# One Perceiver layer on one core: the heads' content stored by single tiles, the exponential's table loaded later, eleven zero products, one rounding moved

## The reference

```python
x = x + xattn(layernorm(x), ctx)      # Q = x Wq' + bq, K = ctx Wk' + bk, softmax(Q K'/32) ctx; ctx has 4096 rows
x = x + attn(layernorm(x), ...)       # 128 heads of 8, latent 128, rope part of 64
x = x + ffn(layernorm(x), W1, b1, W2, b2)

# attn
c_q = x @ Wq_down;  c_kv = x @ Wkv_down
q_c = (c_q @ Wq_up).reshape(b, s, 128, 8);  q_r = (x @ Wq_rope).reshape(b, s, 128, 64)
k_c = (c_kv @ Wk_up).reshape(b, s, 128, 8); v_c = (c_kv @ Wv_up).reshape(b, s, 128, 8)
k_r = x @ Wk_rope
scores = (einsum(q_c, k_c) + einsum(q_r, k_r)) / sqrt(72)
out = (softmax(scores) @ v_c).reshape(b, s, 1024) @ Wo

# ffn: two of these, W1 of 4096 x 1024 and W2 of 1024 x 4096
outlier = max(abs(x), axis=rows) > 3
y = quant_rows(where(outlier, 0, x)) @ quant_rows(W).T + where(outlier, x, 0) @ W.T + b
# quant_rows: scale = max(max|row|/127, 1e-8); round(a/scale) * scale
```

## Time and profile before

| | |
|---|---|
| median of three runs | 924.37 us (923.29 to 924.41) |
| profiled execution, whole time | 925.35 us |
| its span in the profile | 923.3 us |
| busy: PE, PEld | 895.4 us (97%), 818.6 us (89%) |
| busy: DVE, ACT, POOL | 684.6, 627.3, 488.9 us (74, 68, 53%) |
| mean granted PE clock | 0.994 |

### The profile page before, as it was taken

How to read it: one execution, slowest core, us unless ns; L and a number is a source line. 1 busy time by engine, 2 the same in 40 slices (tenths; PEclk the granted TensorE clock), 3 DMA queues, 4 the chain that set the end, 5 groups by cost and what they waited for, 6 DMA issues and landing times.

```text
span 923.3 us, 19052 instructions
## 1 busy us (share of the span) xinstructions
PE 895.4 (97%) x6866; PEld 818.6 (89%) x6866; DVE 684.6 (74%) x1090; ACT 627.3 (68%) x1093; POOL 488.9 (53%) x334
## 2 busy tenths in 40 slices
PE   8999999999999899999999999999899999999997
PEld 6997888888887789999999999987689999899997
DVE  6447676768456468888888888996888888887754
ACT  5424444465444568888888888986678787878762
POOL 0220000045443797777778777773176676376673
PEclk9999999999999999999999999999999999999999
DMA  8566756678754779566565655556232433224221
GB/s 327 190 206 237 293 207 273 249 267 318 275 202 147 221 228 307 174 195 193 179 190 177 213 176 190 176 192 199 93 137 97 178 128 145 92 93 164 109 92 46
DMA packets 80696, 174.82 MB, mean 189 GB/s; under 512 B 7632, under 2 KB 57584, under 8 KB 78064
## 3 DMA queue, kind: packets, MB, share of 16 engines
q1 hardware_dynamic: 79920, 173.63, 53.8%
q10 hardware_dynamic: 704, 0.23, 0.1%
HBM read 161.51 MB, written 11.53 MB: 187 GB/s over the span
## 4 chain that ended last, share of the span: by engine, by line
PE 73%; DVE 6%; ACT 4%; POOL 3%; issue 2%; DMA 2%; SPq 0%; DVEq 0%; ACTq 0%; POOLq 0%
PE bank L51 17%; PE bank L53 17%; PE bank L52 17%; PE bank L1408 4%; PE bank L1409 3%; PE bank L549 3%; PE bank L1379 3%; PE bank L1804 2%; PE bank L2089 2%; PE bank L1424 2%; POOL W_all L2328 1%; DMA ring<-in_L_attn_Wq_rope_dram 1%; POOL wl L1003 1%; PE bank L1391 1%; PE bank L731 1%
## 5 line engine op out<-in xcount | busy, mean ns | idle before, releaser
L1003 POOL TENSOR_TENSOR wl<-ring,wh 128x1024 fp32r<-128x1024 f32 x68 | 161.9, 2402 | 0.0
L51 PE MATMUL bank<-act_all,W_all 128*128 128x256 f32 (+1 forms) x512 | 154.0, 301 | 2.3 <-POOL W_all L2328 1.9
L51 PE MATMUL bank<-act_all,wh 128*128 128x256 f32 x512 | 144.5, 282 | 1.3 <-DVE qq L1609 0.9
L52 PE MATMUL bank<-act_all,wh 128*128 128x256 f32 x512 | 144.1, 281 | 0.0
L53 PE MATMUL bank<-act_all,W_all 128*128 128x256 f32 (+1 forms) x512 | 144.0, 281 | 0.0
L53 PE MATMUL bank<-act_all,wl 128*128 128x256 f32 x512 | 143.8, 281 | 0.0
L513 POOL TENSOR_TENSOR xa_WT_l<-ring,xa_WT_h 128x1024 fp32r<-128x1024 f32 x16 | 43.4, 2732 | 176.6 <-ACT xa_WT_h L508 166.7
L2328 POOL TENSOR_TENSOR W_all<-rnd,W_all 128x512 fp32r<-128x512 f32 x72 | 92.3, 1292 | 57.4 <-ACT W_all L2215 52.1
L1616 DVE TENSOR_TENSOR pl<-bank,ph 128x512 f16<-128x512 f32 x128 | 88.1, 688 | 44.4 <-ACT ph L1555 41.6
L1000 POOL CAST wh<-ring 128x1024 fp32r<-128x1024 f32 x68 | 68.8, 1041 | 69.5 <-PE bank L53 62.2
L51 PEld LDWEIGHTS bank<-act_all,W_all 128*128 128x128 f32 x512 | 97.1, 190 | 3.4 <-POOL W_all L2328 2.5
(11 more groups left out here) (275 smaller groups left out, 2604.2 us busy)
## 6 DMA issues: line engine op xcount, KB each, us to landing
ring<-in_ctx_dram SPq DMA_DIRECT2D x16, 2048.0 KB, 8.1
ring<-in_L_attn_Wq_rope_dram SPq DMA_DIRECT2D x32, 1024.0 KB, 6.4
ring<-in_L_ffn_W_dram SPq DMA_DIRECT2D x14, 2048.0 KB, 7.7
panel<-in_L_ffn_W_dram SPq DMA_DIRECT2D x48, 512.0 KB, 4.6
w1p<-in_L_ffn_W_dram SPq DMA_DIRECT2D x16, 512.0 KB, 3.7
ring<-in_L_xattn_Wq_dram SPq DMA_DIRECT2D x2, 2048.0 KB, 12.5
ring<-in_L_xattn_Wk_dram SPq DMA_DIRECT2D x2, 2048.0 KB, 7.8
ring<-in_L_attn_Wo_dram SPq DMA_DIRECT2D x4, 1024.0 KB, 5.0
```

Source lines behind the costliest of these rows:

```text
L51: pe.matmul(out, lh, rh, start=start, stop=False, skip_group_check=True)
L52: pe.matmul(out, lh, rl, start=False, stop=False, skip_group_check=True)
L1003: pool.tensor_tensor(half_of(l, i), half_of(r, i), f32(half_of(h, i)), ALU.subtract).then_inc(w_lo, 1)
```

## The change

Four edits.

1. Content. Before the heads only the keys of buffer 0 are spread, and only the first tile of q and of k is stored (`store_tiles`, 128 KB a DMA). SP then reads group 0's content back, spreads the other two buffers, stores the second tile (on a semaphore of its own, for which group 4 waits), and only then loads piece 2 of Wq_rope.
2. The exponential's table is loaded behind the copies of the values.
3. Zero products in layer norm 3: 3 become 8 ahead of the first turned rows, 6 become 10 ahead of the masked rows, 5 become 7 ahead of the scaled rows.
4. First W1 step: DVE scales chunk 0's results one rounding later; ACT biases them behind k = 6 and 7, by a table of its own.

```diff
@@ content_sync and what it calls
+            stored_left = sem("stored_left")
+            def store_tiles(sp, i, tiles, done):
                 for s in range(SLOTS):
                     part = con_l if s == 2 - i else con_h
                     sp.dma_start(content_dram[i][tiles, s * P:(s + 1) * P, :].rearrange("t p q -> p t q"),
-                                 f32(part[i][:, tiles, :])).then_inc(stored[u], 16)
+                                 f32(part[i][:, tiles, :])).then_inc(done, 16)
+            def store_content(sp, u, i):
+                sp.wait_ge(con_lo, 2 * u + i + 1)
+                store_tiles(sp, i, slice(2 * u, 2 * u + 2), stored[u])
...
                     sp.wait_ge(kr_hi, 2)
-                    for b in range(QBUF):
-                        sp.dma_start(f32(kmix[0:ROPE, b * GROUP:(b + 1) * GROUP, :]),
-                                     f32(krope[0:ROPE, 1, :]).unsqueeze(1).to_broadcast([ROPE, GROUP, T])).then_inc(k_spread, 16)
+                    spread_keys(sp, 0)
                     for i in range(2):
-                        store_content(sp, 0, i)
-                    sp.wait_ge(k_spread, QBUF * 16)
+                        sp.wait_ge(con_lo, i + 1)
+                        store_tiles(sp, i, slice(0, 1), stored[0])
@@ content_scalar
-                    load_exp(act, ident[:, 0:1])
                     act.wait_ge(e_ready, 1)
...
                             act.activation(value_part(kt, h, 0), by_head(bank[2 * kt + h][:, :]), ACT.Copy).then_inc(v_hi, 1)
+                    load_exp(act, ident[:, 0:1])
@@ heads_sync
                         if g % 8 == 0:
                             sp.wait_ge(stored[g // 8], 2 * SLOTS * 16)
+                        elif g == 4:
+                            sp.wait_ge(stored_left, 2 * SLOTS * 16)
...
-                    next_w(2)
+                    sp.wait_ge(k_spread, 16)
+                    sp.wait_ge(cleared, 2 * QBUF + 1)
                     for g in range(FIRST, NG):
...
                         if valid(g + 2):
                             content(g + 2)
+                        if g == FIRST:
+                            for b in (1, 2):
+                                spread_keys(sp, b)
+                            for i in range(2):
+                                store_tiles(sp, i, slice(1, 2), stored_left)
+                            next_w(2)
+                            sp.wait_ge(k_spread, QBUF * 16)
@@ feed-forward tables, zero products, first step
-            TILES_AT_FIRST = ((), (), (), (), (0, 1), (2,), (3,), ())
+            TILES_AT_FIRST = ((), (), (), (), (), (0, 1), (2,), (3,))
+            BIASED_AT_FIRST = ((), (), (), (), (), (), (0,), (1, 2, 3))
...
-                        keep_warm(pe, 4, 3)
+                        keep_warm(pe, 4, 8)
...
-                        keep_warm(pe, 2, 6)
+                        keep_warm(pe, 2, 10)
                         for h in range(2):
                             pe.wait_ge(y_masked, 4 + 4 * h)
...
-                        keep_warm(pe, 2, 5)
+                        keep_warm(pe, 2, 7)
                         pe.wait_ge(m_max, 2 * QT)
...
-                    step(0, 0, None, None, first=True, tiles=TILES_AT_FIRST)
+                    step(0, 0, None, None, first=True, tiles=BIASED_AT_FIRST)
```

6 lines of the change are left out of this document (3 added, 3 removed).

## The result

The changed kernel takes **928.25 us** (median of six runs, 927.5 to 930.06), the kernel before beside it 924.39 us (six runs, 922.1 to 925.3): ratio 1.0047, 95% interval 1.0035 to 1.0058, so 3.9 us slower. Two repeats gave 1.0044 (1.0027 to 1.0061) and 1.0037 (1.0024 to 1.005). The forecast was 923.6 us with a range of 920.6 to 926.6; the result lies above it.

A forecast was written before the change was run, and what follows sets the result against it. PE, busy nearly throughout, was taken as the bound. Content +2.3, layer norm 3 -0.9 and W1 -2.2 sum to -0.8: profiled 925.35 becomes 924.55, or 923.6 us after the profiled run's 0.98 above the median; range 920.6 to 926.6.

The forecast's parts named there:

- Table: Start of the heads: without the exponential's table load ahead, PE starts the content products at 303.1 instead of 303.60, 0.5 us less.
- Content: Heads' start: the new transfer order delays the end of POOL's chain from 341.68 to 344.0, +2.3 us, between -0.2 and +4.7.
- POOL's chain of 20.6 us: Heads: fixed-order POOL work from Wq_rope piece 2's landing (321.05) to PE's restart (341.68), 20.6 us, sets the stage.
- The landing of w2: Heads: Wq_rope piece 2 (w2) lands at 323.4 instead of 321.05; bounds 320.9 and 325.8.
- The sum, 322.5: Heads: start of data movement at 312.2 plus transfer times of content, two spreads, six stores and Wq_rope piece 2 gives 322.5.
- the lag behind it: Heads: time from the summed transfers to Wq_rope piece 2's landing, taken as 0.9 us; it was 3.3 before.
- a new stretch at 0.50 behind 320: Sign anywhere behind 320 us: a new stretch at granted clock 0.50 would mean the prediction is wrong.
- PE's waits, 2 to 3 us in sum: Heads, 327 to 344: PE waits 2 to 3 us in sum for POOL's low part or group 1's content.
- rival B: Heads: Wq_rope piece 2 lands late, 1 us per us after 321.05; 926.0 us, with low clock 927.7; chance 0.15.
- rival A: Heads: transfers hidden, Wq_rope piece 2 lands at 321 or before; 921.1 us, 919.2 if at 319 or before; chance 0.26.
- Layer norm 3: Layer norm 3: added zero products hold the clock and DVE's 0.94 us wait goes, -0.9 us; bounds 0 and -0.94.
- W1: First W1 product: moved rounding, -0.85 from PE's wait, -1.65 from clock, +0.3 later maxima: -2.2 us; bounds -0.5 and -2.5.

The follow-up runs named there:

- after_again: The changed kernel itself, run again with a second profile: 927.77 us, ratio 1.0044 to the kernel before.
- w2_first: The changed kernel with Wq_rope piece 2 issued directly behind group 0's content, ahead of two spreads and the second tile's stores: 929.6 us, ratio 1.004.
- zeros_only: The kernel before with only layer norm 3's zero products changed: 924.17 us, ratio 0.9998.
- no_content: The changed kernel with the content's transfers as before, the other three edits kept: 922.89 us, ratio 0.997; its repeat 923.04 us, ratio 0.9992.
- w2_behind_content0: The kernel before, two-tile stores kept, with Wq_rope piece 2 issued behind group 0's content and SP's wait for the stores: 926.72 us, ratio 1.0025.
- w2_mid: The changed kernel with Wq_rope piece 2 issued behind the two spreads, ahead of the second tile's six stores: 925.22 us, ratio 0.9995.
- content_only: The kernel before with only the content's transfers changed: 928.31 us, ratio 1.0034; its repeat 928.17 us, ratio 1.0044.
- keys_then_content1: The changed kernel, order behind group 0's content: Wq_rope piece 2, two spreads, wait for keys, group 1's content, second tile's stores: 925.68 us, ratio 1.0012.
- content1_w2_late: The changed kernel with group 1's content ahead of the second tile's stores and Wq_rope piece 2 behind them: 930.28 us, ratio 1.0066.

## Why the prediction was wrong

**Table** (-0.5 at the content products, hidden behind POOL). Right in the changed kernel: 304.00 with 0.52 idle, load and exponential at 315.23 inside ScalarE's gap, and no measurable change of the time by itself. That it also brings w2 forward in the old order was not seen.

**Content** (+2.3, bounds -0.2 to +4.7). This step failed, by its size: +4.72 in the trace, 2.9 to 6.0 over the twelve traces in which SP waits with the queues running dry. The mechanism held: no wait before the first scores, POOL's chain of 20.6 us behind w2 as the setter, 1 us of PE for each us of w2. The +4.72 are 3.81 by w2, 1.09 with the lower clock, and -0.18 behind that. Two things were mis-sized.
- The landing of w2, 323.4. It was cast at 325.76, which is 324.9 when the 0.90 ahead of the change is taken off (after_again: 323.87 + 0.51 = 324.4). The sum, 322.5, was added up from the earlier trace rows; what failed is the lag behind it, taken as 0.9 where 2.4 were measured, "nearer to the stores, since the queues are not full for as long". The row of w2 itself had 3.3. What makes this lag no run shows. The sum's own start for w2, 318.5, was met, though by two errors that cancel: the first stores had landed at 309.8 instead of 311.1, and SP took longer over the rest, since behind the two spreads the six 128 KB stores took 5.5 us to issue. w2 was issued at 318.35 and used 7.4 us later. And a load isn't faster for having little ahead: w2_first issued it at 311.32 with 0.2 MB ahead; by the sum's terms it lands at 317.0 (1.1 + 0.6 + 4.0 later), and POOL got it at 320.64.
- The lower clock was in no term of the sum. It came for 3.41 us behind the last wait and cost 1.09 us. The prediction had named a new stretch at 0.50 behind 320 as a sign that it is wrong, and the stretch stands at 345.5.

Group 1's content, which the text named and did not price, was late as well (1.67 us), but inside the wait for POOL, so it cost nothing here. Once w2 is early it does: 3.97 us in w2_first. What was expected as PE's waits, 2 to 3 us in sum, measured 6.74 for the same reason: PE was ahead and waited three times for the one delay.

The outcome was rival B, with its place, its price of 1 us for each us, its condition (from 324.15 on slower) and its total (926.0, with the clock 927.7). It had 0.15, against 0.46 for w2 at 322 to 324.5. Of rival A, 919.2 was out of reach: w2's cast also waits for PE, which still reads `wh`, and in no trace is the cast more than 1.63 us earlier than before, where 2.1 were counted.

**Layer norm 3** (-0.9): -0.86 in the trace, and as stated: the clock stood at 1.00 and DVE's 0.94 us went. But they also went in three of seven traces with the old zero products, so the price holds only against an execution with the fall; against the median of the runs zeros_only gave 0.2 us. That the sum came right there is the luck of the profiled execution. **W1** (-2.2): -1.34; the wait of 0.92 us became 0.18, that of 0.69 went, that of 0.27 grew to 0.62, and about 0.95 of the gain is the fall that was not there, priced at 1.65. Both rested on one execution of before that had two falls at once; a pair of falls takes 3.7 thousandths from the mean clock (3.41 us at half, of 923), and some runs of before have 0.999. The three edits together, priced at 3.1, measured 2.8 us (1.9 to 3.6) and 0.7 us (-0.5 to 1.9) in no_content and its repeat.

**Tail**: +0.63, in no term.

Against the forecast's profiled sum of -0.8 the trace has +3.67: 2.42 from the content, 0.04 and 0.86 from layer norm 3 and W1, 0.25 from what follows them (-0.15 + 0.63 - 0.23), 0.90 from ahead of the change.

The Trainium skill ("DMA: Bandwidth & Descriptors", Queues, rings and completion order) says that each DMA engine consumes its ring in order but that transfers need not complete in order. Read alone, the first half would make a load that is issued first independent of what follows; w2 took 9.3 us from issue to use ahead of the spreads (w2_first) and 8.9 behind them (w2_mid, 311.45 to 320.33), so no run here shows that being first helps.

## What to carry to other kernels

Look for the transfer behind which a fixed chain of work stands, and price a new order of transfers by when that one lands: here the heads followed it 1:1, and moving this one issue ahead of six stores took the ratio from 1.0037 to 1.0047 down to 0.9995. A wait that is put ahead of it costs the same way (w2_behind_content0), and so does the issuing engine's own time over small stores. Take the lag between a sum of bytes and a landing from the row of the same transfer, not from a more convenient one. Waits in sum are not a loss: several can stand for one delay, and only the last counts. Then look for the second gate, which takes over when the first is early. Read a clock's fall from one execution as a chance, not as a cost that an edit can remove: compare the mean clock over many runs, and ask whether the profiled execution is a typical one.

## What the runs showed of the hardware

- Whether the clock falls can differ although PE did the same ahead of it. In all seven traces with the old zero products PE was busy 1.79 or 1.80 us of the 3.50 that begin with these products (in before 649.3 to 652.8); the clock then fell in four and not in three. In the thirteen with the new ones it was busy 2.93 to 2.95 us there, and the clock fell in none. content_only and the changed kernel:

```profile
652.65:656.15 3.50, 1.79 (x12) 1.00 0.00 0
```

```profile
655.00:658.50 3.50, 2.94 (x17) 1.00 0.00 0
```

  In all four traces with a fall in layer norm 3 a second one began 37.5 us later, and in no other trace with the old rounding.
- A stretch of 3.4 us at a clock of 0.50, with PE busy, put the heads back by 0.75 to 1.12 us where nothing waited behind it, and by nothing where PE had to wait afterwards anyway.
- SP took 1.30 and 1.43 us to issue three stores of 128 KB, 4 us behind one spread, 3.00 and 2.46 us behind two spreads just issued. A 1 MB load took 6.9 to 9.4 us from issue to use, with 0.2 MB ahead of it (w2_first, 9.3) as with more.
- Spreads of 1 KB pieces issued just behind a 1 MB load took 11.2 us to land (keys_then_content1, 310.36 to 321.56), without it (content1_w2_late, 311.51 to 316.33) 4.8 us.
- The load of the exponential's table took 1.28 us.
